# Probabilities of the second attention turned by VectorE in 32x32 blocks and passed through DRAM, instead of by TensorE

## What is computed

```python
q = jnp.einsum('bsd,hpd->bhsp', x, q_w.reshape(H, P, D))
k = jnp.einsum('bsd,hpd->bhsp', x, k_w.reshape(H, P, D))
xv = jnp.einsum('bsd,hedp->bshep', x, v_w.reshape(H, E, D, P))
v = jnp.einsum('bshep,bshe->bhsp', xv, gate_v)
att = jax.nn.softmax(jnp.einsum('bhqp,bhkp->bhqk', q, k) * SCALE, axis=-1)
ctx = jnp.einsum('bhqk,bhkp->bqhp', att, v)
weighted = ctx[:, :, :, None, :] * gate_o[..., None]
out = jnp.einsum('bshep,hepd->bsd', weighted, o_w.reshape(H, E, P, D))
```

## Time and profile before

| | |
|---|---|
| runs | 3132.07, 3137.17, 3143.18 us |
| median | 3137.17 us |
| profiled execution: its own time (the span from first to last instruction) | 3102.4 us |
| instructions | 53,399 |
| TensorE busy | 2958.3 us (95%) |
| VectorE | 2183.4 us (70%) |
| ScalarE | 1926.7 us (62%) |
| GpSimd | 1838.9 us (59%) |
| DMA queue of SP and ACT | 88.75 MB in 127,312 packets |
| mean granted TensorE clock | 0.979 |

### The profile page before, as it was taken

The page is one execution under the profiler, slowest core; times in us unless marked ns, Lnnn a source line. Parts: engine busy times, 40 slices in busy tenths (PEclk is TensorE's granted clock), DMA queues, the critical chain, the costliest instruction groups (busy, mean ns, idle before and its releaser), DMA issues. The chain is left out here.

```text
span 3102.4 us, 53399 instructions
## 1 busy us (share of the span) xinstructions
PE 2958.3 (95%) x17672; PEld 2071.1 (67%) x17672; DVE 2183.4 (70%) x4152; ACT 1926.7 (62%) x4366; POOL 1838.9 (59%) x2333
## 2 busy tenths in 40 slices
PE   4999999999999999999999999999999987899998
PEld 2666666666666666666666666666667675567675
DVE  7777888877778888777788887777777655235243
ACT  1576666676667666666666666666666743353634
POOL 2466666676666666676766676666666645433330
PEclk7899999999999999999999999999999989899999
DMA  5000001100100011001000110011001011233222
GB/s 171 21 22 23 22 22 33 32 23 26 44 26 22 23 32 33 23 23 37 29 22 22 33 32 23 23 37 29 23 22 40 16 42 44 65 96 104 86 77 87
DMA packets 140048, 124.71 MB, mean 40 GB/s; under 512 B 28662, under 2 KB 122304, under 8 KB 139680
## 3 DMA queue, kind: packets, MB, share of 16 engines
q1 hardware_dynamic: 127312, 88.75, 10.2%
q0 software_dynamic: 10160, 30.17, 3.1%
q10 hardware_dynamic: 2304, 2.36, 0.4%
HBM read 97.47 MB, written 29.28 MB: 41 GB/s over the span
## 5 line engine op out<-in xcount | busy, mean ns | idle before, releaser
L1340 DVE TENSOR_REDUCE m_peaks<-m_ring 128x1 f32<-128x512 f32 x1024 | 636.7, 681 | 95.3 <-PE m_ring L299 95.1
L1072 ACT ACTIVATE m_expA<-m_ring 128x512 f32<-128x512 f32 x1024 | 536.3, 607 | 120.5 <-PE m_ring L372 102.3
L933 POOL TENSOR_TENSOR m_vprod<-m_vprod 128x512 f32<-128x512 f32 x256 | 334.3, 1306 | 451.5 <-DVE m_vprod L1353 327.1
L1043 ACT ACTIVATE m_prob<-m_ring,m_negs 128x512 f32<-128x512 f32 x512 | 350.8, 691 | 285.9 <-DVE m_negs L1388 285.4
L943 POOL TENSOR_TENSOR m_oprod<-m_oprod 128x512 f32<-128x512 f32 x256 | 329.4, 1287 | 258.9 <-ACT m_oprod L1012 255.2
L350 PE MATMUL m_ring<-m_probT,m_vs 128*128 128x256 f32 x2048 | 464.4, 380 | 5.8 <-DVE m_vprod L1353 5.2
L350 PEld LDWEIGHTS m_ring<-m_probT,m_vs 128*128 128x128 f32 x2048 | 386.3, 190 | 68.4 <-issue 13.3
L1378 DVE TENSOR_REDUCE m_negs<-m_ring 128x1 f32<-128x512 f32 x512 | 344.3, 684 | 115.3 <-PE m_ring L105 113.2
L1353 DVE TENSOR_TENSOR m_vprod<-m_ring,m_gate 128x512 f32<-128x512 f32 x512 | 342.2, 687 | 112.4 <-PE m_ring L105 99.5
L1053 ACT ACTIVATE m_probT<-m_ring 128x512 f32<-128x512 f32 x512 | 294.0, 610 | 63.2 <-PE m_ring L338 61.8
L1012 ACT ACTIVATE m_oprod<-m_ring,m_go 128x128 f32<-128x128 f32 x1024 | 292.0, 372 | 34.6 <-PE m_ring L105 23.7
(11 more groups left out here) (322 smaller groups left out, 5558.3 us busy)
## 6 DMA issues: line engine op xcount, KB each, us to landing
m_wraw<-in_v_w SPq DMA_DIRECT2D x32, 512.0 KB, 4.1
m_qf<-q_dram SPq DMA_DIRECT2D x128, 128.0 KB, 2.7
m_wraw<-in_o_w SPq DMA_DIRECT2D x32, 512.0 KB, 4.3
q_dram<-m_kf SPq DMA_DIRECT2D x24, 256.0 KB, 4.4
listed<-in_pad SPq DMA_DIRECT2D x6, 897.0 KB, 11.5
m_xg<-listed SPq DMA_DIRECT2D x39, 138.0 KB
m_rows<-answers SPq DMA_DIRECT2D x8, 512.0 KB, 4.1
sums_dram<-m_sumsT ACTq DMA_DIRECT2D x128, 18.0 KB
```

Source lines behind the costliest of these rows:

```text
L933: vchain(pool.tensor_tensor(vprod[:, 0:512], vprod[:, 0:512], vprod[:, 512:1024], ALU.add))
L1043: act.activation(prob[t % 2][:, c * 512:(c + 1) * 512], ring.home["scores", n, t, c][:, :], ACT.Exp, bias=neg[t % 2], accum_out=den[n % 2] ...
L1072: act.activation(expA[hh][:, c * 512:(c + 1) * 512], ring.home["scT", n, k, hh, c][:, :], ACT.Exp)\
L1340: v.tensor_reduce(peaks[:, t, hh, c:c + 1], ring.home["peaks", n, t, hh, c][:, :], AX.X, ALU.max)\
```

## The change

TensorE's `turn` and ScalarE's `keep_turned` are gone. VectorE's `turn_probs` transposes the probabilities of a query tile ([128, 1024]) in blocks of 32 x 32 into `turned`. A block transpose stays within 32 partitions, so 32 consecutive keys of one tile of 128 still lie on the partitions of the queries' block. SP puts them right through DRAM: `store_probs` writes `turned` of a pair of tiles to `probs_dram` (128 rows of 8 KB, two buffers), and `load_probs` reads it back with four loads of 256 KB. Load c takes the 32 rows of query block c; each row holds four blocks of 2 KB, and the load reads the blocks in the order block, row ("r b q -> b r q"), 4 x 32 x 512 elements on the DRAM side, and writes 512 elements to each of the 128 partitions. `probT` and `turned` have one buffer each. The columns of the context then stand in the order (block, tile, query), which `by_tile` and `by_block` put right in `keep_ctx` and `lower_ctx`.

The lists of all engines are in a new order (`range(-5, N0 + 5)`), the peak and key scores of a tile come four at a time, and SP's transfers stand in one loop with the new ones. `probs_turned` now counts tiles. Three further edits move nothing in a head: `scale_outputs` takes the half c as an argument (always 1), the early heads' sums are fetched in two functions, and a semaphore of the weights' split is shared.

```diff
+def by_tile(half):
+
+    return half.rearrange("p (t a j) -> p a t j", t=2, a=4)
+
+
+def by_block(ps):
+
+    return ps[:, 0:2 * P].rearrange("p (a t j) -> p a t j", a=4, t=2)
+
...
-        probT = [m.sbuf(f"probT{k}", [P, TPB, 2 * P]) for k in range(2)]
+        probT, turned = m.sbuf("probT", [P, 4, TPB, 64]), m.sbuf("turned", [P, 4, TPB, 2, 32])
...
+        probs_stored, probs_moved = m.sems("probs_stored probs_moved")
+        probs_dram = [nc.dram_tensor(f"probs_dram{k}", (P, 4, 512), F32, kind="Internal").ap() for k in range(2)]
...
-                def turn(n, t, h):
-                    if n not in steps:
-                        return
-                    pe.wait_ge(probs_made, 2 * (TPB * n + t) + h + 1)
-                    ps = claim(ring, ("probT", n, t, h), probT_kept, 16 * n + 2 * t + h + 1)
-                    for c in range(4):
-                        last = pe.transpose(ps[:, c * P:(c + 1) * P],
-                                            prob[t % 2][:, (4 * h + c) * P:(4 * h + c + 1) * P], ident[:, :])
-                    last.then_inc(probs_turned, 1)
-
                 def weigh(n, g):
                     if n not in steps:
                         return
                     if g == 0:
                         pe.wait_ge(v_ready, TPB * (n + 1))
-                    pe.wait_ge(probT_kept, 16 * n + 4 * g + 4)
+                    pe.wait_ge(probs_moved, 16 * LOADS * (4 * n + g + 1))
                     ps = claim(ring, ("ctx", n, g), ctx_ready, 4 * n + g + 1)
                     for k in range(TPB):
-                        last = pe.matmul(ps[:, 0:2 * P], vs[n % 2][:, k, :], probT[g % 2][:, k, :],
+                        last = pe.matmul(ps[:, 0:2 * P], vs[n % 2][:, k, :], probT[:, :, k, :],
                                          start=(k == 0), stop=(k == TPB - 1))
                     last.then_inc(ctx_made, 1)
...
                     weigh(i - 1, 0)
+                    make_y(i, 0)
+                    scores_by_key(i - 1, 4)
                     sum_by_key(i - 1, 3)
-                    scores_by_key(i - 1, 4, 0, 0)
-                    scores_by_key(i - 1, 4, 0, 1)
-                    scores_by_key(i - 1, 4, 1, 0)
-                    scores_by_key(i - 1, 4, 1, 1)
                     values(i, 5, 0)
-                    turn(i - 1, 4, 0)
                     values(i, 5, 1)
-                    turn(i - 1, 4, 1)
-                    peak_scores(i, 5, 0, 0)
-                    peak_scores(i, 5, 0, 1)
-                    peak_scores(i, 5, 1, 0)
-                    peak_scores(i, 5, 1, 1)
+                    peak_scores(i, 5)
                     sum_by_key(i - 1, 4)
-                    scores_by_key(i - 1, 5, 0, 0)
-                    scores_by_key(i - 1, 5, 0, 1)
-                    scores_by_key(i - 1, 5, 1, 0)
-                    scores_by_key(i - 1, 5, 1, 1)
+                    scores_by_key(i - 1, 5)
                     values(i, 6, 0)
                     values(i, 6, 1)
                     scores(i - 1, 6, 0)
-                    peak_scores(i, 6, 0, 0)
-                    peak_scores(i, 6, 0, 1)
-                    peak_scores(i, 6, 1, 0)
-                    peak_scores(i, 6, 1, 1)
                     scores(i - 1, 6, 1)
                     weigh(i - 1, 1)
-                    scores_by_key(i - 1, 6, 0, 0)
-                    scores_by_key(i - 1, 6, 0, 1)
-                    scores_by_key(i - 1, 6, 1, 0)
-                    scores_by_key(i - 1, 6, 1, 1)
+                    peak_scores(i, 6)
                     sum_by_key(i - 1, 5)
-                    turn(i - 1, 5, 0)
+                    scores_by_key(i - 1, 6)
                     values(i, 7, 0)
+                    values(i, 7, 1)
+                    peak_scores(i, 7)
+                    scores(i - 1, 7, 0)
+                    scores(i - 1, 7, 1)
                     outputs(i - 1, 0, 0)
-                    values(i, 7, 1)
-                    turn(i - 1, 5, 1)
-                    turn(i - 1, 6, 0)
                     outputs(i - 1, 0, 1)
-                    peak_scores(i, 7, 0, 0)
-                    peak_scores(i, 7, 0, 1)
-                    peak_scores(i, 7, 1, 0)
-                    peak_scores(i, 7, 1, 1)
+                    batch_work(i - 2, 2)
                     sum_by_key(i - 1, 6)
-                    turn(i - 1, 6, 1)
-                    scores(i - 1, 7, 0)
+                    scores_by_key(i - 1, 7)
+                    batch_work(i - 2, 3)
+                    scores(i, 0, 0)
                     outputs(i - 1, 1, 0)
-                    scores(i - 1, 7, 1)
-                    batch_work(i - 2, 2)
-                    outputs(i - 1, 1, 1)
-                    scores(i, 0, 0)
                     scores(i, 0, 1)
-                    batch_work(i - 2, 3)
-                    weigh(i - 1, 2)
-                    scores_by_key(i - 1, 7, 0, 0)
-                    scores_by_key(i - 1, 7, 0, 1)
-                    scores_by_key(i - 1, 7, 1, 0)
-                    scores_by_key(i - 1, 7, 1, 1)
-                    turn(i - 1, 7, 0)
-                    turn(i - 1, 7, 1)
                     scores(i, 1, 0)
                     scores(i, 1, 1)
+                    weigh(i - 1, 2)
                     turn_peaks(i, 0)
+                    turn_peaks(i, 1)
+                    outputs(i - 1, 1, 1)
+                    values(i + 1, 0, 0)
+                    values(i + 1, 0, 1)
                     outputs(i - 1, 2, 0)
+                    scores(i, 2, 0)
+                    scores(i, 2, 1)
                     outputs(i - 1, 2, 1)
-                    turn_peaks(i, 1)
-                    turn(i, 0, 0)
-                    values(i + 1, 0, 0)
                     outputs(i - 1, 3, 0)
-                    scores(i, 2, 0)
-                    turn(i, 0, 1)
-                    values(i + 1, 0, 1)
-                    scores(i, 2, 1)
                     outputs(i - 1, 3, 1)
                     weigh(i - 1, 3)
-                    turn(i, 1, 0)
...
+                def store_probs(n, g):
+                    if n not in steps:
+                        return
+                    k = 4 * n + g
+                    sp.wait_ge(probs_turned, 2 * k + 2)
+                    if k >= 2:
+                        sp.wait_ge(probs_moved, 16 * LOADS * (k - 1))
+                    sp.dma_start(probs_dram[k % 2].rearrange("p b q -> p (b q)"),
+                                 turned[:, :, :, :, :].rearrange("p b k t j -> p (b k t j)")).then_inc(probs_stored, 16)
+
+                def load_probs(n, g):
+                    if n not in steps:
+                        return
+                    k = 4 * n + g
+                    sp.wait_ge(probs_stored, 16 * (k + 1))
+                    if k:
+                        sp.wait_ge(ctx_made, k)
+                    for c in range(4):
+                        sp.dma_start(probT[:, c, :, :].rearrange("p k q -> p (k q)"),
+                                     probs_dram[k % 2][32 * c:32 * c + 32, :, :].rearrange("r b q -> b r q")).then_inc(probs_moved, 16)
...
+                for i in range(-5, N0 + 5):
+                    load_probs(i - 1, 1)
+                    batch_loads(i - 1)
+                    store_probs(i - 1, 2)
+                    load_probs(i - 1, 2)
+                    load_values(i + 1)
+                    store_probs(i - 1, 3)
+                    load_probs(i - 1, 3)
+                    load_queries(i + 1)
+                    store_probs(i, 0)
+                    load_outputs(i)
+                    load_probs(i, 0)
+                    store_probs(i, 1)
...
-                        act.wait_ge(probs_turned, 2 * (k - 2) + c + 1)
+                        act.wait_ge(probs_turned, k - 1)
...
-                def keep_turned(n, t, h):
-                    if n not in steps:
-                        return
-                    g = 4 * n + t // 2
-                    act.wait_ge(probs_turned, 16 * n + 2 * t + h + 1)
-                    if g >= 2:
-                        act.wait_ge(ctx_made, g - 1)
-                    act.activation(probT[g % 2][:, 4 * h:4 * h + 4, (t % 2) * P:(t % 2 + 1) * P],
-                                   ring.home["probT", n, t, h][:, :].rearrange("p (c q) -> p c q", c=4),
-                                   ACT.Copy).then_inc(probT_kept, 1)
...
-                    act.activation(ctxT[g % 2][:, 0, :].bitcast(F32R), ring.home["ctx", n, g][:, 0:2 * P], ACT.Copy).then_inc(ctx_upper, 1)
+                    act.activation(by_tile(ctxT[g % 2][:, 0, :].bitcast(F32R)), by_block(ring.home["ctx", n, g]), ACT.Copy).then_inc(ctx_upper, 1)
...
+                def turn_probs(n, t):
+                    if n not in steps:
+                        return
+                    k = TPB * n + t
+                    v.wait_ge(probs_made, 2 * k + 2)
+                    if t % 2 == 0 and k:
+                        v.wait_ge(probs_stored, 16 * (k // 2))
```

(3 more changed lines are left out.)

## The result

The changed kernel takes 3624.51 us (median of 4 runs, 3615.2 to 3630.53) against 3136.73 us: a ratio of 1.155, 95% interval 1.1528 to 1.1572. The direction was forecast, the size was not: 3428 us, range 3035 to 3550. The profiled execution's span is 3623.6 us.

The account below looks back on a forecast made before the run. TensorE, 99% busy at 75.1 us a head, was taken as the bound. Work 67.4, stalls 12.5 and clock 3.4 made 83.3 us; with extra terms +291 us on 3137.2 gave 3428 us, range 3035 to 3550.

Parts of the forecast that it names:

- Four engines, 13.2 us a pair: Loads of turned probabilities: four outermost blocks mean four DMA engines carry a pair's 1 MB, landing in 13.2 us.
- Stalls of 12.5 us a head: TensorE waiting for loads before weighings 1, 2 and 3: 4.7, 1.3 and 6.5 us, together 12.5 us a head.
- Transposes of 1.2 us on VectorE: Eight block transposes a head on VectorE at 1.2 us each, 9.6 us, bringing VectorE to 68.4 us a head.
- Clock, 3.4 us a head: TensorE after the two long stalls: lowered clock makes the work 1.7 us longer each time, 3.4 us a head.
- A head: 67.4 + 12.5 + 3.4 = 83.3 us: Head period: TensorE's work without transposes, plus load stalls, plus clock; 8.2 us more than now, +254 us over 31 periods.
- Rival B: Loads spread over all engines, 5.2 us, no stalls; 72 us a head, 3041 us (2960 to 3110); chance 0.24.
- The attention sums, 8 us in three heads: SP issues the attention sums' loads between pair 1's loads and pair 2's store: 8 us in each of three heads, +25.
- The last head, 12 us: In the last head TensorE has no values and peaks to put between the weighings: some 12 us more.
- Median to span, 34.8 us: The runs' median stands 34.8 us above the profiled span; the forecast left that difference as it was.
- Rival D: Stalls as forecast, but faster engines (loads 11.5 us) and the clock kept up: head 75.2 us, 3160 us; chance 0.06.
- The forecast's growth of 291 us: Whole kernel: 254 us from 31 head periods, 25 from the attention sums and 12 from the last head.

Follow-up runs that it names:

- the doses of two and sixteen engines: The changed kernel with each load split by pairs of key blocks (two engines): 4784.9 us; with loads cut by key block (sixteen): 3136.44 us.
- Filling the stalls: The changed kernel with 16 and 26 idle TensorE products ahead of the load waits at weighings 1 and 3: 3579.63 us, ratio 1.1389.
- The run with the long fills: The changed kernel with 32 and 52 idle TensorE products ahead of the load waits at weighings 1 and 3: 3703.78 us, ratio 1.1774.
- the loads by key block: The changed kernel with a pair's four loads cut by key block, 32 rows outermost on both sides: 3136.44 us, ratio 0.9977.

## Why the prediction was right in kind and wrong in size

- **Four engines, 13.2 us a pair: right in kind, a little low.** A DMA share of 0.25, and the doses of two and sixteen engines. From the first issue to the weighing it was 12.95 us in the example; over heads 3 to 29 the medians are 13.5, 14.0 and 14.5 us for pairs 1, 2 and 3.
- **Stalls of 12.5 us a head: right.** The trace has 443.3 us in all, 36.5 of them behind the last split: (443.3 - 36.5) / 31 = 13.1 a head.
- **Transposes of 1.2 us on VectorE: right**, and VectorE was not the bound.
- **Clock, 3.4 us a head: too little for the slow products, too much for what they cost.** The weighings behind the two long stalls take 6.05 and 5.7 us instead of 3.6, 4.5 us a head. Filling the stalls gave back 1.2: 2.0 in the stretch 1 to 2, and nothing in 3 to 0, where waits for other engines took its place.
- **"A head: 67.4 + 12.5 + 3.4 = 83.3 us": the step that failed,** first of all in its 67.4 us of TensorE's work. The mechanism held, the sizes did not: a steady head takes 89.0. The run with the long fills leaves 70.5 us for the work. Between weighing 3 and the next 0 the forecast had 25 us, and that run has 31.25 - 3.6 = 27.6: the 23 tiles take 0.77 us each and not 0.72, the nine groups of peak and key scores 0.58 and not 0.5. Where the loads end a stretch, this doesn't count. By the table, the 5.7 us that are missing are 1.8 of work in the last stretch, 2.1 of loads in the other three (13.5, 14.3 and 14.5 us from the end of one weighing to the start of the next, for 13.2, 13.2 and 13.8), and 1.8 of longer weighings. In the kernel before, taking 5.1 us of TensorE's work gave 1.8: at 99% busy it was still not alone in setting the pace. Rival B rested on the same 67.4 us: its 72 us were 74.3. Steady heads grew by 13.2 us (75.7 to 89.0, the sums of the medians), not by 8.2; over the 31 periods the difference is 148 us, the attention sums included.
- **The attention sums, 8 us in three heads: about right.** Those heads took 101.2, 99.8 and 106.9 us against 75.0, 79.7 and 81.4 before: 13.0, 6.9 and 12.3 above the steady growth, 32 us for 25.
- **The last head, 12 us: too little.** Five stalled weighings lie behind the last split of the queries, not one head's extra work: 36.5 us of idleness, and 13.9 us more for the weighings at the lower clock. That is 50 us, 38 more than forecast.
- **Median to span, 34.8 us: left as it was, rightly, by luck.** It was read as what timing from outside adds; that is 2 us. It is about the size of the hole, which I could not know.
- **Rival D's sum** doesn't come out: 0.1 us a head and the 37 us of extra terms on 3137 make 3177 us, not 3160. Nothing rests on it.

The forecast's growth of 291 us and these corrections, 148 and about 40, make some 480 us; the medians differ by 487.8.

## What to carry to other kernels

An engine that is 99% busy is not proof that its work can be priced one for one. Where others are at 78% and hand over through few buffers, leave a part of the work out in a trial run before the gain is counted; in the kernel before, a third came through. For a DMA, look at the outermost count on both sides before anything else: a cut along another axis made the same four loads four times as wide. And compare the profiled execution with the median of the runs: a gap of 1% here was, as it seems, a wait of its own.

## What was not expected of the hardware

With all engines at work, the loads by key block moved 213 to 250 GB/s at a DMA share of about 1, where transfers over 128 rows had reached 399. The pieces are of 2 KB in both; each of these loads writes 32 partitions. No run tells whether that is the reason. It did not matter here, as a pair still landed before its weighing in most cases.

The second is the hole: GpSimd's indirect transfers, one every 1.26 us and 28 in a row, went with 38 us of idleness on ScalarE in the traces without spaced transfers, that of before excepted, and a wait after every two or four of them took it away, for about 0.8% of the time.
